# Second attention of a fused block: weights transposed in halves of 64 tokens, and another order of the work on TensorE, VectorE and ScalarE

## What is computed

```python
q = proj(query, Wq, bq); k = proj(key, Wk, bk); v = proj(value, Wv, bv)
scores = einsum('bhqd,bhkd->bhqk', q, k) * scale + rel_bias
attn = softmax(scores)
out = einsum('bhqk,bhkd->bhqd', attn, v)
out = out.transpose(0, 2, 1, 3).reshape(b, tq, DIM) @ Wo + bo
x = x + tanh(g_xattn) * out
```

## Time and profile before

| | value |
|---|---|
| runs | median 464.58 us (463.58 to 464.70) |
| the profiled execution: its time, its span | 460.31 us, 458.5 us |
| TensorE busy / weight loads busy | 412.8 us (90%) / 295.2 us (64%) |
| VectorE, ScalarE, GpSimd busy | 323.7 us (71%), 251.9 us (55%), 128.3 us (28%) |
| chain that ended last, by engine | PE 59%, DVE 20%, issue 3%, DMA 3%, ACT 2% |
| mean granted TensorE clock | 0.943 |

### The profile page before, as it was taken

One profiled execution on the slowest core, in us unless ns is written; L12 is line 12 of the kernel. 1 busy time (PEld: TensorE's weight loads), 2 busy tenths in 40 slices (PEclk: granted clock), 3 DMA queues, 4 the chain that ended last, 5 costly groups with the idle time before them and its releaser, 6 DMA issues.

```text
span 458.5 us, 7476 instructions
## 1 busy us (share of the span) xinstructions
PE 412.8 (90%) x2436; PEld 295.2 (64%) x2437; DVE 323.7 (71%) x661; ACT 251.9 (55%) x420; POOL 128.3 (28%) x143
## 2 busy tenths in 40 slices
PE   8999999999997129999999999996987999999993
PEld 8887744444434028878877768874866576767762
DVE  3999984459998998964776887778356465555652
ACT  3563755479998975412487767775541623424210
POOL 5623155000000350421196000100123645351222
PEclk9998999999997558999999999998897999999998
DMA  7920000000002014000399000000064312120000
GB/s 238 294 4 0 1 3 0 0 0 0 0 0 62 1 21 91 1 0 0 101 390 414 16 1 2 0 1 2 1 173 138 105 55 66 52 60 33 27 21 1
DMA packets 27424, 27.25 MB, mean 59 GB/s; under 512 B 11611, under 2 KB 23586, under 8 KB 27139
## 3 DMA queue, kind: packets, MB, share of 16 engines
q1 hardware_dynamic: 25187, 21.73, 15.4%
q0 software_dynamic: 2208, 5.14, 3.8%
HBM read 22.63 MB, written 5.15 MB: 61 GB/s over the span
## 4 chain that ended last, share of the span: by engine, by line
PE 59%; DVE 20%; issue 3%; DMA 3%; ACT 2%; POOL 1%; DVEq 0%; POOLq 0%; ACTq 0%
PE quad L1666 24%; PE bank L1666 24%; PE bank L1959 5%; DVE amP L1369 3%; DVE big_g L1400 2%; PE bank L2154 2%; DMA token_rows<-x_rows 2%; DVE big_g L485 2%; DVE mx L1496 2%; PE quad L1710 1%; DVE big_g L1494 1%; DVE big_g L1497 1%; DVE amZ L1303 1%; DVE amU L1309 1%; PE bank L1975 1%
## 5 line engine op out<-in xcount | busy, mean ns | idle before, releaser
L1666 PE MATMUL quad<-yT,ffn_w 128*128 (+1 forms) x128 | 56.3, 593 | 0.0
L767 ACT ACTIVATE big_u<-bank 77x512 f32<-77x512 f32 (+2 forms) x72 | 39.2, 592 | 12.8 <-PE bank L1959 12.0
L1065 ACT ACTIVATE yT<-yT 128x512 f32<-128x512 f32 x23 | 14.5, 631 | 52.2 <-DVE yT L1621 52.2
L1666 PEld LDWEIGHTS quad<-yT,ffn_w 128*128 128x128 f32 x128 | 24.0, 190 | 29.5 <-issue 28.3
L1666 PE MATMUL quad<-big_g,yT 128*128 x92 | 41.8, 595 | 0.5 <-ACT yT L767 0.5
L1666 PE MATMUL bank<-big_u,yT 128*128 x184 | 41.8, 380 | 0.2 <-DVE yT L1635 0.2
L1959 PE MATMUL bank<-ident,big_g 128*77 128x128 f32 x256 | 36.4, 288 | 2.2 <-ACT big_g L992 1.9
L744 POOL DMA_INDIRECT out<-yT,k_blockdiag x23 | 23.3, 1013 | 50.8 <-DVE yT L1635 47.5
L1666 PEld LDWEIGHTS bank<-big_u,yT 128*128 128x128 f32 x184 | 34.1, 190 | 5.0 <-issue 0.9
L1621 DVE TENSOR_TENSOR yT<-quad,ffn_w 128x512 f32<-128x512 f32 x23 | 15.9, 692 | 25.5 <-PE quad L1666 25.5
L1959 PEld LDWEIGHTS bank<-ident,big_g 128*77 128x77 f32 x256 | 29.4, 153 | 7.0 <-ACT big_g L992 3.3
(11 more groups left out here) (320 smaller groups left out, 925.5 us busy)
## 6 DMA issues: line engine op xcount, KB each, us to landing
big_g<-in_L_ffn_W SPq DMA_DIRECT2D x1, 4096.0 KB, 13.5
big_u<-in_L_ffn_W SPq DMA_DIRECT2D x1, 4096.0 KB, 24.8
x_rows<-in_x SPq DMA_DIRECT2D x4, 512.0 KB, 6.7
ffn_w<-in_L_ffn_b SPq DMA_DIRECT2D x1, 2048.0 KB, 26.3
tmp<-bias_by_distance SPq DMA_DIRECT2D x2, 616.0 KB, 7.3
token_rows<-x_rows SPq DMA_DIRECT2D x1, 1032.0 KB, 11.2
tmp<-in_L_ffn_b SPq DMA_DIRECT2D x1, 1024.0 KB, 6.2
token_rows<-x_rows SPq DMA_DIRECT2D x1, 774.0 KB, 11.6
```

The lines of the kernel that those rows point to most:

```text
L767: act.activation(out_, in_, ACT.Copy, **k).then_inc(done, 1)
L1065: act.activation(hb[:, u, :], hb[:, u, :], ACT.Gelu).then_inc(s.gelu_sb, 1)
L1666: return pe.matmul(out_, lhsT=lhsT, rhs=rhs, start=first, stop=last)
```

## The change

`weightsT` becomes 16 transposes of 64 tokens each. Tokens 0 to 63 use rows 0 to 63 of the array and write bank 6, tokens 64 to 127 use rows 64 to 127 and write bank 7; the two alternate. A unit waits for both copies of the unit before it, where it waited for each bank's own. ScalarE's copies scatter each bank into pT in runs of 64 elements. The order of the calls changes in every `pair(t)`, and with it the place of some waits; `token_back` swaps banks 4 and 5, and waits before the second one until ScalarE has read the queries from bank 4.

```diff
--- before.py
+++ after.py
@@ -460,6 +460,7 @@
 
         LAST = NT - 2
         PLACES = (0, 2, 1, 3)
+        HP = P // 2
 
         def position(t):
 
@@ -974,9 +975,10 @@
 
 
             def weightsT(t, ci, u):
+                places = pT.rearrange("k (a c h) n -> k a c h n", a=2, c=CH)[:, :, ci, :, :]
                 for k in range(2):
-                    o = PLACES[2 * ci + k] * HQ
-                    copy(pT[:, o:o + HQ, u * P:(u + 1) * P], pb[6 + k][0:KEYS, :].rearrange("k (h p) -> k h p", h=HQ),
+                    o = u * P + k * HP
+                    copy(places[:, :, :, o:o + HP], pb[6 + k][0:KEYS, :].rearrange("k (a h n) -> k a h n", a=2, h=HQ),
                          s.pT_ps, 2 * (2 * t + 2 * ci + u) + k + 1, s.pT_sb)
 
             def heads_out(t, ci):
@@ -993,33 +995,35 @@
 
             def pair(t):
                 if t:
-                    weightsT(t - 2, 1, 0)
-                    if t >= 4:
-                        attended(t - 4)
-                    else:
-                        y3_out_late(NQB - 1, 0)
-                    weightsT(t - 2, 1, 1)
-                    if t < 4:
-                        y3_out_late(NQB - 1, 1)
+                    heads_out(t - 2, 0)
                 exponents(t, 0, 0)
                 if t == 0:
                     y3_out_late(NQB - 2, 0)
                     y3_out_late(NQB - 2, 1)
+                if t == 2:
+                    y3_out_late(NQB - 1, 0)
+                if t >= 4:
+                    attended(t - 4)
+                if t:
+                    weightsT(t - 2, 1, 0)
                 exponents(t, 0, 1)
+                if t == 2:
+                    y3_out_late(NQB - 1, 1)
                 if t:
+                    weightsT(t - 2, 1, 1)
                     heads_out(t - 2, 1)
+                exponents(t, 1, 0)
                 weightsT(t, 0, 0)
-                weightsT(t, 0, 1)
-                exponents(t, 1, 0)
+                exponents(t, 1, 1)
                 if t < LAST:
                     queries(t + 2)
-                exponents(t, 1, 1)
-                heads_out(t, 0)
+                weightsT(t, 0, 1)
 
             for t in range(0, NT, 2):
                 pair(t)
+            heads_out(LAST, 0)
+            attended(LAST - 2)
             weightsT(LAST, 1, 0)
-            attended(LAST - 2)
             weightsT(LAST, 1, 1)
 
             def y4T_out(k):
@@ -1458,7 +1462,7 @@
             def head_out(t, u):
 
                 dve.wait_ge(s.o_ps, t + u + 1)
-                o = pb[u if t == LAST else 5 + u][:, 0:H * VE].rearrange("p (h d) -> p h d", d=VE)
+                o = pb[u if t == LAST else 5 - u][:, 0:H * VE].rearrange("p (h d) -> p h d", d=VE)
                 c.link(dve.reciprocal(rd[:, u, :], o[:, :, HD]))
                 dve.tensor_tensor(att[:, u, :].rearrange("p (h d) -> p h d", d=HD), o[:, :, 0:HD],
                                   rd[:, u, :].unsqueeze(2).to_broadcast([P, H, HD]), ALU.mult).then_inc(s.att_sb, 1)
@@ -1522,8 +1526,8 @@
                     residual(t - 4, 1)
                     moments(t - 4)
                 unit(t, 1, 0)
+                unit(t, 1, 1)
                 head_out(t - 2, 0)
-                unit(t, 1, 1)
                 head_out(t - 2, 1)
 
             first_pair()
@@ -1949,18 +1953,22 @@
             def weightsT(t, ci, u):
                 n = 2 * t + 2 * ci + u
                 pe.wait_ge(s.e_exp, n + 1)
-                for k in range(2):
-                    if n:
-                        pe.wait_ge(s.pT_sb, 2 * (n - 1) + k + 1)
-                    if (ci, u, k) == (1, 0, 0) and t:
-                        pe.wait_ge(s.att_sb, t)
-                    for h in range(HQ):
-                        o = (2 * ci + k) * HQK + h * KEYS
-                        ins = pe.transpose(pb[6 + k][0:KEYS, h * P:(h + 1) * P], e_[:, u, o:o + KEYS], ident[:, :])
-                    ins.then_inc(s.pT_ps, 1)
+                if n:
+                    pe.wait_ge(s.pT_sb, 2 * n)
+                for h in range(HC):
+                    o = ci * HCK + h * KEYS
+                    for k in range(2):
+                        half = slice(k * HP, (k + 1) * HP)
+                        ins = pe.transpose(pb[6 + k][0:KEYS, h * HP:(h + 1) * HP], e_[half, u, o:o + KEYS], ident[half, half])
+                        if h == HC - 1:
+                            ins.then_inc(s.pT_ps, 1)
 
             def heads(t, ci):
                 pe.wait_ge(s.pT_sb, 2 * (2 * t + 2 * ci + 1) + 2)
+                if ci:
+                    pe.wait_ge(s.oT_sb, t + 1)
+                elif t:
+                    pe.wait_ge(s.att_sb, t - 1)
                 for k in range(2):
                     for g in range(HQ):
                         h = (2 * ci + k) * HQ + g
@@ -1970,15 +1978,15 @@
 
             def token_back(t, u):
 
-                ps = pb[u if t == LAST else 5 + u]
+                ps = pb[u if t == LAST else 5 - u]
                 for hq in range(NQ):
                     ins = pe.transpose(ps[:, hq * P:(hq + 1) * P], oT[:, hq, u * P:(u + 1) * P], ident[:, :])
                 ins.then_inc(s.o_ps, 1)
 
             def project_in(t):
 
+                pe.wait_ge(s.att_sb, t + 2)
                 for u in range(2):
-                    pe.wait_ge(s.att_sb, t + u + 1)
                     for ci in range(CH):
                         ins = pe.transpose(pb[5 if t == LAST else 4][:, (CH * u + ci) * P:(CH * u + ci + 1) * P],
                                            att[:, u, ci * P:(ci + 1) * P], ident[:, :])
@@ -2019,36 +2027,34 @@
 
                 if t:
                     fill(t, 0)
-                    weightsT(t - 2, 1, 0)
+                    heads(t - 2, 0)
                     if t >= 4:
                         project_in(t - 4)
                     else:
                         y3_late(NQB - 1, 0)
-                    weightsT(t - 2, 1, 1)
+                    weightsT(t - 2, 1, 0)
                     if t >= 4:
                         project(t - 4)
                     else:
                         pe.wait_ge(s.y3T_sb, 11)
                         y3_late(NQB - 1, 1)
-                    pe.wait_ge(s.oT_sb, t - 1)
+                    weightsT(t - 2, 1, 1)
+                    fill(t, 1)
                     heads(t - 2, 1)
-                    fill(t, 1)
                 weightsT(t, 0, 0)
+                if t == 2:
+                    pe.wait_ge(s.y3T_sb, 12)
+                if t >= 4:
+                    pe.wait_ge(s.x3_done, t - 2)
+                if t < LAST:
+                    queries(t + 2)
+                weightsT(t, 0, 1)
                 if t:
                     pe.wait_ge(s.oT_sb, t)
                     token_back(t - 2, 0)
-                weightsT(t, 0, 1)
-                if t == 2:
-                    pe.wait_ge(s.y3T_sb, 12)
-                if 4 <= t < LAST:
-                    pe.wait_ge(s.x3_done, t - 2)
-                if t < LAST:
-                    queries(t + 2)
-                if t:
-                    pe.wait_ge(s.pT_sb, 2 * (2 * t + 1) + 1)
+                    if t < LAST:
+                        pe.wait_ge(s.q_sb, t + 4)
                     token_back(t - 2, 1)
-                    pe.wait_ge(s.att_sb, t - 1)
-                heads(t, 0)
 
             first_fills()
             for t in range(0, NT, 2):
@@ -2079,14 +2085,13 @@
                 pe.wait_ge(s.lT_sb, g + 1)
                 pe.transpose(pb[1][:, g * P:(g + 1) * P], lT[:, g, :], ident[:, :]).then_inc(s.lg_ps, 1)
 
+            heads(LAST, 0)
+            project_in(LAST - 2)
             weightsT(LAST, 1, 0)
-            pe.wait_ge(s.x3_done, LAST - 2)
-            project_in(LAST - 2)
+            project(LAST - 2)
             weightsT(LAST, 1, 1)
             y4_in(0)
             y4_in(1)
-            project(LAST - 2)
-            pe.wait_ge(s.oT_sb, LAST + 1)
             heads(LAST, 1)
             y4_in(2)
             y4_in(3)
```

## The result

The changed kernel takes 481.18 us in the median of its four executions, the kernel before 464.08 beside it. The ratio is 1.0335 (95% interval 1.0297 to 1.0373), some 3.4% slower. The profiled execution took 482.78 us with a span of 481.0, against 460.31 and 458.5; the other two took 477.09 and 479.58.

What follows compares the result with a forecast made beforehand. TensorE alone bounded the middle pairs of the second attention; the new order was to make waits through ScalarE and VectorE longer. Terms 1.5 + 0.9 + 4.4 + 2.4 + 2.4 + 1.5 = 13.1 us gave 477.5 us, range 471 to 484.

Steps and rivals of the forecast that it cites:

- The ring: Second attention, steady pair: longest way round through TensorE, VectorE and ScalarE takes 13.4 us instead of 12.31, +1.1 us a pair.
- TensorE's own work: Steady pair: faster transposes less added changes of array shape leave TensorE's work only 0.3 us lower, at 12.0 us.
- The start: Scores of t = 2 begin at 233.05 instead of 231.53 us, queries standing behind an exponent: +1.5 us.
- pair 6: Pair with the bias of near positions, three of four units on the ring: 15.9 against 13.44 us, +2.4.
- the end: Pair 14 and what ends it: copies and heads behind a waiting exponent, last projection followed by more transposes: +2.4 us.
- Pair 2: Pair t = 2, no projection yet: the same waits, partly under VectorE's spare time: +0.9 us.
- The term of the clock: Granted clock: one further fall near 232 us and a longer one at the end: +1.5 us, bounds 0 and +5.
- halves do not overlap: Rival: each transpose waits for the other's rows, ring 1.0 us longer in pairs not VectorE's, about 484 us; chance 0.11.
- Faster, nothing new waits: Rival: exponent ahead of `attended` costs nothing, TensorE sets the pair at 12.0 us, 462.5 us in all; chance 0.08.

Runs made afterwards that it cites:

- e3: Changed kernel with `attended` moved ahead of the exponent of unit (t, 0, 0) on ScalarE: 474.08 us, ratio 1.0298.
- e4: e3 with ScalarE's exponents of the second half also moved behind the copies of (t, 0, 0) and (t, 0, 1): 462.68 us, ratio 1.0071.
- e8: Changed kernel with ScalarE's copies and `attended` ahead of the exponents throughout, and 5 idle matmuls ahead of the scores of t = 2: 465.11 us, ratio 1.002.
- e7: Same as e8 but with full transposes in place of halves: 462.24 us, ratio 1.0004.
- e5: Changed kernel with all 8 halves of rows 0 to 63 first, then those of rows 64 to 127: 489.28 us, ratio 1.057.
- e6: Changed kernel with idle matmuls, 4 ahead of unit (0, 0, 1) and 5 ahead of the scores of t = 2: 476.73 us, ratio 1.0299.
- e10: e6 with 22 more idle matmuls in the hole of the last pair, t = 14: 474.25 us, ratio 1.0301.
- e2: Changed kernel with 8 full transposes of 128 tokens and the old copies, new order and wait for both copies kept: 473.76 us, ratio 1.0293.
- e9: e7 without its idle matmuls ahead of the scores of t = 2: 461.73 us, ratio 0.9982.

## Why the prediction was right, and where not

The median came out at 481.18 us for 477.5, within the range. (The prediction's own terms give 473.4 + 4.3 = 477.7; the 0.2 is a slip of its sum.) Without the execution of 1036.8 us the median rose by 15.5 us for the 13.1 forecast. On the profiled executions, for which the sum was made, the result is +22.5. So the mechanism was right, while the number owes something to luck: the sum falls 9.4 us short there, 4.6 us by the clock at pair 2 and 4.9 us outside the attention, and it is the other two executions, 3.2 and 5.7 us shorter, that bring the median near. The steps one by one:

- **The ring.** Right, and nearly to the number: 13.4 us forecast, 13.44 measured; the projection begins 3.79 us after the scores (3.73), the residual 5.90 (5.85), the exponent 9.79 (9.7), unit (t, 0, 1) 11.62 (11.45). e3 takes the first link out and e4 the second, and the pair falls to 12.78 and 12.33. The waits of TensorE were forecast at 0.8, 0.5 and 0.2 to 0.3 us, and measured at 0.70, 0.43 and 0.28.
- **TensorE's own work.** Right: 0.3 us less a pair forecast, 0.28 (changed kernel) to 0.34 us (e8 against e7) measured, a round of two halves 0.069 us (in the trace the rounds of the unit at 301.22 start at 301.405, 301.474 and 301.543) for 0.065. e5 settles that the halves overlap. The Trainium skill, "TensorEngine Tiling (Array Packing)", Theoretical Speedup, allows up to 2x for 64 rows. Here the unit went from 0.92 to 0.70 us, 1.3x, and TensorE's own work for a pair from 12.24 to 11.90, 1.03x.
- **The start, pair 6, the end.** Forecast +1.5, +2.4 and +2.4; measured +1.6, +2.5 and +2.0. That ScalarE's order makes the first two is shown by e4 (13.33 and 12.89 us). The near-equal end conceals a fall of 6.8 us on both sides, so that the agreement of this term says little; the fall there was also forecast to be longer than the one before, and was not.
- **Pair 2 and the clock.** Pair 2 by itself was sized well: +0.9 forecast, +0.7 at full clock (e6, 12.15). The term of the clock failed: "+1.5, with bounds 0 and +5". The place was right, near 232 us. The price was not: it took 6.1 us there alone. The prediction gives the 1.5 us no working. The one fall that its rows show was 6.8 us long, with TensorE busy for 4.92 of them; this one lasted 17.1 us, over a stretch in which TensorE hardly waits and its work takes 1.7 to 1.9 times as long (1.30 us for 0.77, 3.78 for 1.99).
- **The rest, +4.9 us outside the attention**, was in no term ("the experts' stage behind it only starts later"): +1.1 ahead of it, in code that is the same, and +3.7 behind. Of these, 2.9 us are the two unexplained waits in the experts' stage.

The rivals: "halves do not overlap" is refuted. e5 comes nearest to it and takes 0.25 us more a pair, not 1.0; by the prediction's own walk, with one of four units on the ring, it would have been 0.5. "Faster, nothing new waits" needed less than 0.3 us of idle TensorE in a pair; there are 1.41. The orders of ScalarE that were tried do not reach it either: e4 and e8 stand at 12.33, not 12.0, because of the wait of 0.43 us for the two copies.

## What to carry to other kernels

Before work is moved to make one engine faster, walk the longest way round through all engines, with a duration from the trace for each hand-over: here it gave the new pair to 0.04 us, and named the two instructions of ScalarE (an exponent ahead of a tile that TensorE waits for) that made the loss. In an in-order queue, put the result that another engine waits for ahead of the one that can wait. And price a new hole on TensorE by the dense work behind it, not by the hole alone: waits of 1.68 and 1.97 us cost another 6.1 us at low clock, and nine calls of a matmul that no one reads took this back at that place. Whether a hole brings a fall can't be read from the hole: the same 1.61 us ahead of the last projection had none in the changed kernel and one in e6 and e10.

## What the runs showed of the hardware that was not expected

Once the granted clock had fallen to 0.50 near 232 us, it stayed there 13.7 to 17.1 us in four kernels with transposes of 64 rows, and 3.4 to 6.8 us in two with full ones, although TensorE is listed as busy nearly all the time in all of them (2.93 to 3.40 us of every 3.4; 3.40 of the 3.4 us from 234.4 us on in both the changed kernel and e2, which differ in the form of the transposes alone). What in the halves does it was not tested, and the falls at the end of the attention show this difference less clearly (e9 above). Half a clock also does not touch all work alike: at 0.50 a unit of halves lasts 1.30 us for 0.77, and eight matmuls of 256 columns 3.78 for 1.99. Half the rows do not make a weight load shorter: with 77 columns it takes 160 ns in the mean for 64 rows and 153 ns for 128. Whether the loads are what limits a round of two halves was not tested.
